# Attention sums stored unturned and normalised later; part of the row maxima copied out of PSUM by ScalarE

## The reference

```python
def _L0_attn_ref(x, Wq, Wk, Wv, bv, Wo, bo):
    ...
    q = _rope(q)
    k = _rope(k)
    scores = jnp.einsum('bhsd,bhtd->bhst', q, k) * scale
    causal = jnp.triu(jnp.ones((S, S), dtype=bool), k=1)
    scores = jnp.where(causal, -jnp.inf, scores)
    probs = jax.nn.softmax(scores, axis=-1)
    out = jnp.einsum('bhst,bhtd->bhsd', probs, v)
    out = out.transpose(0, 2, 1, 3).reshape(B, S, HID)
    return jnp.einsum('bsh,eh->bse', out, Wo) + bo

def _L0_ffn_ref(x, W_fc, W_proj):
    ...
    h = jnp.square(jax.nn.relu(jnp.einsum('bsd,fd->bsf', x, W_fc)))
    y = jnp.einsum('bsf,df->bsd', h, W_proj)
    ...
    _, spks = jax.lax.scan(step, mem0, None, length=NUM_STEPS)
    return jnp.sum(spks, axis=0) / NUM_STEPS
x = L0_attn_x
x = x + 0.5 * _L0_ffn_ref(_layernorm(x, axis=-1), L0_ffn_W_fc, L0_ffn_W_proj)
x = x + _L0_attn_ref(_layernorm(x, axis=-1), L0_attn_Wq, L0_attn_Wk, L0_attn_Wv, L0_attn_bv, L0_attn_Wo, L0_attn_bo)
x = x + 0.5 * _L0_ffn_ref(_layernorm(x, axis=-1), L0_ffn_W_fc, L0_ffn_W_proj)
```

## Time and profile before

| | |
|---|---|
| time, median of 3 runs | 1481.79 us (1480.66 to 1482.88) |
| the profiled execution | 1480.84 us, span 1479.1 us |
| PE, DVE, ACT busy | 1345.1, 1134.0, 861.4 us |
| attention's exponentials | from 405 to 1250 us; a group from 1 to 6 takes 106.0 us |

### The profile page before, as it was taken

How to read it: one execution, slowest core, us unless ns; L and a number is a source line. 1 busy time by engine, 2 the same in 40 slices (tenths; PEclk the granted TensorE clock), 3 DMA queues, 4 the chain that set the end, 5 groups by cost and what they waited for, 6 DMA issues and landing times.

```text
span 1479.1 us, 22638 instructions
## 1 busy us (share of the span) xinstructions
PE 1345.1 (91%) x8416; PEld 809.8 (55%) x8416; DVE 1134.0 (77%) x2686; ACT 861.4 (58%) x1157; POOL 223.7 (15%) x205
## 2 busy tenths in 40 slices
PE   4988888967799999999999999999999998999996
PEld 3877777854444343444444444443443433999996
DVE  6566776796788888898898898888888851576675
ACT  4654455511166666676666666666666668665664
POOL 4002222241210110110110110110210110101100
PEclk9999999976699999999999999999999999999998
DMA  3123443772272160250340420610701011232312
GB/s 110 48 81 119 136 135 122 149 209 93 72 109 29 27 92 6 39 75 6 56 59 6 75 40 5 91 24 5 106 9 44 9 33 47 76 100 87 99 44 72
DMA packets 98598, 101.41 MB, mean 69 GB/s; under 512 B 39260, under 2 KB 78940, under 8 KB 96860
## 3 DMA queue, kind: packets, MB, share of 16 engines
q1 hardware_dynamic: 98488, 99.97, 29.7%
HBM read 60.16 MB, written 37.75 MB: 66 GB/s over the span
## 4 chain that ended last, share of the span: by engine, by line
PE 74%; DVE 19%; ACT 4%; issue 3%; DMA 0%; POOL 0%; SPq 0%; DVEq 0%; ACTq 0%
PE m_ps L1049 20%; PE o_ps L1094 18%; DVE maxes L971 9%; PE yps_c L563 6%; PE ups_c L545 6%; PE s_ps L1078 5%; PE ups_a L545 5%; PE yps_a L563 4%; PE gps_a L594 3%; DVE masked L974 3%; PE gps_a L579 2%; DVE turned_a L403 2%; PE gps_c L579 2%; ACT probs L950 1%; PE tps_a L572 1%
## 5 line engine op out<-in xcount | busy, mean ns | idle before, releaser
L950 ACT ACTIVATE probs<-s_ps 128x1024 f32<-128x1024 f32 (+3 forms) x640 | 542.0, 896 | 282.6 <-PE s_ps L1078 281.2
L971 DVE TENSOR_REDUCE maxes<-m_ps 128x1 f32<-128x512 f32 x768 | 490.2, 684 | 72.6 <-PE m_ps L1049 70.7
L1049 PE MATMUL m_ps<-kT,qT 64*128 64x512 f32 (+3 forms) x1280 | 455.6, 459 | 56.4 <-DVE maxes L971 37.9
L1049 PEld LDWEIGHTS m_ps<-kT,qT 64*128 64x128 f32 x1280 | 204.2, 192 | 412.1 <-DVE maxes L971 277.6
L1078 PE MATMUL s_ps<-qT,kT 64*128 64x512 f32 (+3 forms) x1280 | 317.0, 404 | 6.8 <-ACT probs L950 6.6
L1094 PE MATMUL o_ps<-probs,v_w 128*32 128x512 f32 (+3 forms) x2560 | 311.1, 559 | 0.1
L974 DVE CUSTOM_DVE_ANT_0 masked<-m_ps,mask 128x384 f32<-128x384 f32 (+3 forms) x512 | 233.6, 485 | 52.7 <-PE m_ps L1049 50.8
L919 POOL TENSOR_SCALAR_AFFINE_SELECT probs<-probs 128x512 f32<-128x512 f32 x128 | 81.3, 635 | 742.0 <-ACT probs L950 742.0
L1078 PEld LDWEIGHTS s_ps<-qT,kT 64*128 64x128 f32 x1280 | 170.0, 192 | 34.0 <-ACT probs L950 28.7
L452 DVE TENSOR_TENSOR h_lo_c<-hsq_c,h_hi_c 128x512 fp32r<-128x512 f32 x64 | 45.0, 703 | 71.1 <-ACT hsq_c L301 35.6
L294 ACT ACTIVATE relu_a<-ups_a 128x512 f32<-128x512 f32 x64 | 38.2, 596 | 99.5 <-PE ups_a L545 98.9
(11 more groups left out here) (128 smaller groups left out, 1923.3 us busy)
## 6 DMA issues: line engine op xcount, KB each, us to landing
qT<-qkT_parts SPq DMA_DIRECT2D x96, 128.0 KB
kT<-qkT_parts SPq DMA_DIRECT2D x48, 256.0 KB
qkT_parts<-qk_hi_a SPq DMA_DIRECT2D x32, 256.0 KB, 4.9
qkT_parts<-qk_lo_a SPq DMA_DIRECT2D x32, 256.0 KB, 4.6
table_a<-in_rot SPq DMA_DIRECT2D x8, 768.0 KB, 7.4
xin_a<-in_x SPq DMA_DIRECT2D x8, 512.0 KB, 3.9
xres_a<-in_x SPq DMA_DIRECT2D x8, 512.0 KB, 4.8
x<-xsum_a SPq DMA_DIRECT2D x8, 512.0 KB, 3.2
```

The lines of the kernel that those rows point to most:

```text
L950: act.activation(probs[:, b % PBUF, 2 * hp:2 * hp + 2, off:CH], s_ps[hp][:, :, off:CH], ACT.Exp, scale=D ** -0.5).then_inc(exp_done, 1)
L971: dve.tensor_reduce(out, m_ps[:, i % MB, 0:width], AX.X, ALU.max).then_inc(max_read, 1)
L1049: pe.matmul(m_ps[:, i % MB, 0:width], qT[n % 2][r0:r0 + HR, j, hp, t * P:(t + 1) * P], kT[n % 2][r0:r0 + HR, hp, k * CH:k * CH + width], s ...
```

## The change

**The sums are no longer turned.** ACT copies `o_ps` to one of two halves of `osum`, and three slots after a step's end SP stores them as they are, head by head with queries along the row, to `sumsT`. The 32 ring items of sums go, on PE and on DVE. In the second feed-forward SP loads the denominators of a chunk as 128 x 64 numbers, DVE takes their reciprocals in one instruction (`attn_recip`), SP stores them to `recipT` and loads them back, each row repeated over its head's 16 rows (`denom`), beside the sums (`sums`); DVE multiplies the two (`attn_norm`, 128 x 1024), ACT takes the high part and DVE the low part, now from SBUF. `attn_turn` goes.

**ACT copies half of step 3's plain units.** In groups 1 to 7 the units of step 3 with k = 0 and k = 1 are copied by ACT to `copies` (`copy`, 32 a group, 224 in all); DVE reads both copies of a tile in one instruction over 1024 columns (`copied_pair`), at least two of DVE's own units after the second copy. A bank with such a unit is free once it is copied.

```diff
+COPY = [e for _, e in ORDER if e[0] == "unit" and e[1] > 0 and UNITS[e[2]][0] == NJ - 1 and UNITS[e[2]][4] <= 1]
...
+CBUF = 4
+PAIR_LAG = 2
...
+        def copy(e):
+            i, pair = ITEM[e], PAIR_NO[(e[1],) + UNITS[e[2]][:4]]
...
+            act.wait_ge(max_done, i + 1)
+            if pair >= CBUF:
+                act.wait_ge(max_read, PAIR_READ[PAIRS[pair - CBUF]])
+            act.activation(copies[:, pair % CBUF, UNITS[e[2]][4], :], m_ps[:, i % MB, :], ACT.Copy).then_inc(copied, 1)
...
+            units = [e for e in ITEMS.get(g, []) if e in COPIES]
             for hp in range(2):
+                for e in units[2 * hp:2 if hp == 0 else None]:
+                    copy(e)
                 act.wait_ge(s_done, 2 * g + hp + 1)
...
+        def copied_pair(p):
...
+            both = copies[:, pair % CBUF, :, :].rearrange("p k c -> p (k c)")
+            dve.tensor_scalar(both, both, 0.0, NEG, ALU.add, ALU.max, accum_out=maxes[:, j % 2, par, hp, t, 1:2])\
+               .then_inc(max_read, 1)
...
         def free_bank(e):
-            wait(pe, max_read, ITEM[e] if e in LATE else ITEM[e] - MB + 1)
+            if ITEM[e] >= MB:
+                last = ORDER[ITEM[e] - MB][1]
+                if last in COPIES:
+                    pe.wait_ge(copied, COPIES[last] + 1)
+                else:
+                    pe.wait_ge(max_read, READ[last])
...
-        def turn_sums(e):
...
-        def normalise(e):
...
-        def attn_turn(c):
...
+        def attn_recip(c):
+
+            wait(dve, f"denom_in{c % 2}", 16 * (c // 2 + 1))
+            dve.reciprocal(recip[:, c % 2, :], recip[:, c % 2, :]).then_inc(s["a_recip"], 1)
+
+        def attn_norm(c):
+
+            wait(dve, "a_in", 16 * 2 * EC * (c + 1))
+            dve.tensor_tensor(sums[:, :, :], sums[:, :, :], denom[:, :, :], ALU.mult).then_inc(s["a_norm"], 1)
```

More of the change, by code:

```diff
@@ L101, in feed_forward @@
     else:
-        ain, xb, x2, bias = (own[n] for n in ("ain", "xb", "x2", "bias"))
+        sums, recip, denom, xb, x2, bias = (own[n] for n in ("sums", "recip", "denom", "xb", "x2", "bias"))
         split = [("o", own["stage_o"][:, :], proj_hi, proj_lo)]
@@ L222, in body @@
                     store_x2(it + 1)
+                if has(it, -3):
+                    load_denom(it + 3)
+            elif f == FC - 1 and has(it, -3):
+                store_recip(it + 3)
         def end():
@@ L245, in high, with attn_high @@
                 wait(act, "proj_done", 3 * c)
-            if which == "a":
-                wait(act, "o_done", c)
             act.activation(hi[:, :, :], bank[:, :, :], ACT.Copy).then_inc(s[which + "_hi"], 1)
+        def attn_high(c):
+            wait(act, "a_norm", c + 1)
+            wait(act, "o_done", c)
+            act.activation(mT_hi[:, :, :], sums[:, :, :], ACT.Copy).then_inc(s["a_hi"], 1)
         def v_evac(c):
@@ L663, in body @@
                 up(it, 0)
-            if not first and f == 5 and has(it, -2):
-                attn_turn(it + 2)
         return lead, body
@@ L740 @@
 LAST_UNIT = {(e[1], UNITS[e[2]][0]): e for _, e in ORDER if e[0] == "unit"}
-LATE = [("sums", GROUPS - 1, j) for j in (NJ - 2, NJ - 1)]
-assert [e for _, e in ORDER[-2:]] == LATE
+COPY = [e for _, e in ORDER if e[0] == "unit" and e[1] > 0 and UNITS[e[2]][0] == NJ - 1 and UNITS[e[2]][4] <= 1]
+COPIES = {e: i for i, e in enumerate(COPY)}
+PAIRS = sorted({(e[1],) + UNITS[e[2]][:4] for e in COPY},
+               key=lambda p: max(COPIES[e] for e in COPY if (e[1],) + UNITS[e[2]][:4] == p))
+PAIR_NO = {p: i for i, p in enumerate(PAIRS)}
+CBUF = 4
+PAIR_LAG = 2
+PAIR_AT = {}
+for p in PAIRS:
+    second = max(ITEM[e] for e in COPY if (e[1],) + UNITS[e[2]][:4] == p)
+    at = second + 1
+    lag = 0
+    while lag < PAIR_LAG:
+        lag += ORDER[at][1][0] == "unit" and ORDER[at][1] not in COPIES
+        at += 1
+    PAIR_AT.setdefault(ORDER[at - 1][1], []).append(p)
+READ, PAIR_READ, items_read = {}, {}, 0
+for _, e in ORDER:
+    items_read += e not in COPIES
+    READ[e] = items_read
+    for p in PAIR_AT.get(e, []):
+        items_read += 1
+        PAIR_READ[p] = items_read
 TERMS = [(m, x, par) for m in range(NT) for x in range(2) for par in range(2)]
 LOADS, SHIFTS = 16 * NT * (2 + G) + 32, 16 * 4
-def bank_of(e):
-    return MB - 1 if e in LATE else ITEM[e] % MB
 def place(n):
@@ L822, in moves @@
                     shift(n, j)
-                elif what == "sums":
+            for n, j in steps():
+                if g == min(block_no(n, j, T * j + T) + STORE, LAST):
                     store(n, j)
@@ L1126, in end @@
                 products(*SLOTS[g])
-        def last_sums():
-            ring(ITEMS[LAST])
-        return slot, end, last_sums
+        return slot, end
     return sync, scalar, vector, gpsimd, tensor
```

213 lines of the change are left out of this document (113 added, 100 removed).

## The result

The changed kernel took 1633.0 us (median of 4 runs, 1631.2 to 1633.8), the kernel before 1481.3 in the same comparison: a ratio of 1.102, 95% interval 1.100 to 1.104. The direction is as predicted; 1523 us and its range of 1485 to 1550 are not. The profiled execution took 1632.59 us, span 1630.9.

What follows compares the result with a forecast made beforehand. DVE and PE, handing banks back and forth, bound slots 4 to 19; PE alone bounds the second feed-forward. 1480.8 - 21 (sums, second feed-forward) + 63 (copies) = 1523 us, range 1485 to 1550.

Steps and rivals of the forecast that it cites:

- The pair: Slots 4 to 19: DVE's read of two copies, 1024 columns, costs 1.14 us, saving 0.06 us against two plain maxima.
- Rival A: Slots 4 to 19: pair read at two columns a cycle, copies cost 39 us, kernel 1499 us; chance 0.2.
- ACT's work: Slots 4 to 19: 32 copies add 15.4 us, making 43.3 us against 41.79; 10 us over seven groups.
- ACT over 90% busy: Sign to look for in slots 4 to 19 of groups 1 to 7, with these slots 50 to 52 us long.
- The fours of slots 14 to 19: Slots 14, 16 and 18, all four units copied: four copies cost 1.4 us by the longer loop.
- The longer loop: Chain over pairs through PE and DVE, slots 16 to 18: 6.7 us for two slots against 5.33 before.
- the shorter loop: Chain over ACT, PE and DVE from slot 16's second exponential to slot 18's copy: 6.1 us for two slots.
- The step that failed: Slots 9 and 10 have room for four copies, mixed slots 4 to 8 alternate less; all copies 9 us a group.
- Rival D: Attention: PE gets one more half-speed stretch in each group, 24 us on top, 1547 us; chance 0.08.
- The sums: Attention: 32 ring items go from PE and DVE, 12 us off.
- The second feed-forward: Without attn_turn 7.2 us off, 2 more at group 7's end; DVE's added 1.5 us a chunk covered, otherwise 9 us back.
- Rival B: Slots 4 to 19: copies absorbed in ACT's idle time, only 10 us of throughput added, kernel 1470 us; chance 0.12.

Runs made afterwards that it cites:

- e13: Changed kernel with each copy in ACT's queue where its unit stands in PE's order, and full pair reads two uncopied units later in DVE's queue; 1553.1 us.
- e8: Changed kernel with copies only in slots 12 to 19, 16 a group, part of the units missing from the maxima; 1548.0 us.
- e6: Changed kernel with each copy put into ACT's queue where its unit stands in PE's order; 1605.8 us.
- e14: Changed kernel with only the full pair reads moved two uncopied units later in DVE's queue; 1619.4 us.
- e4: Changed kernel with ACT copying 64 of a unit's 512 columns and DVE reading 128 of a pair's 1024; 1546.9 us.
- e1: Changed kernel without any copies, keeping the unturned sums; 1475.6 us.
- e7: Changed kernel with every unit of scores of groups 1 to 7 computed twice into the same bank; 1672.9 us.
- e5: Changed kernel without copies and with the next tile's norm one step earlier in the second feed-forward; 1462.1 us.
- e12: Changed kernel with only the norm of the tile after next one step earlier in the second feed-forward; 1619.7 us.
- e3: Changed kernel with the read of a pair taking in only 256 columns of each copy; 1626.2 us.

## Why the prediction was right in direction and wrong in size

- **The pair.** Right. The read took 1211 ns and 82 for its accumulator; neighbours start 1.14 us apart (648.93 and 650.07), the price taken. Rival A falls. The rule that the Trainium skill gives in "VectorE: DVE Perf Modes", Mode 2x_2P, does not hold for this form, and the exclusion that the Trainium skill states in "SBUF — State Buffer", "Who interferes with whom", agrees with the measured 1211 ns. `attn_norm` took 1.22 us as priced, the reciprocals 0.55 us where 0.25 was taken.
- **ACT's work.** Right in its sum. The sum of 43.3 us for slots 4 to 19 compares with 26.86 + 16.83 = 43.7 busy in e13. What the prediction wanted to see in the changed kernel, ACT over 90% busy, was not there: 65% in slots 4 to 13. By its own test the step failed there, and e13 shows the state that it had assumed (95%).
- **The fours of slots 14 to 19.** Right in their sum, partly by luck. The longer loop was 6.7 us for two slots; slots 16 and 17 took 6.75 in groups 1 to 7, and 6.21 with half pairs (the shorter loop: 6.1). But in groups 1 to 6 slots 14 and 15 took 7.8 and slots 18 and 19 6.5, and the 5.33 us of before, from which the cost was counted, were the mean of 5.0 and 5.66. Three fours were priced at 3 x 1.4 = 4.2 us, measured 1.9 + 1.7 + 0.9 = 4.5, and e8 shows the same slots up to 2 us longer.
- **The step that failed.** "One of them lies in slots 9 and 10, where the exponentials are narrow and ACT has room ... the mixed slots 4 to 8 alternate less than the others." Slots 4 to 13 were thus priced at about 5 us. They cost 17.8, that is 13 us a group or some 90 of the 110 us missed. Slots 8 to 11, with the four copies of slots 9 and 10 that were to be free, doubled from 7.7 to 15.7 us. Slot 4, counted with the mixed ones, has four copies itself. A mixed slot alternates more, not less: ACT's queue has copies ahead of exponentials whose units come behind the products, and DVE's queue has two reads of pairs ahead of masked maxima that PE needs. I had traced only two loops, in the slots where all four units are alike. e6 and e14 show each of the two orders as a loss in these slots, and e13, with both mended, took 28.3 us in them where the changed kernel took 43.0 and before 25.2. Its sixteen slots, 46.2 to 47.6 us, lie below the 50.8 forecast; what it loses besides lies in slots 20 to 23, for which the prediction had no term.
- **The clock.** Rival D was the right kind: more time at half speed. In slots 4 to 19 the changed kernel had 2 x (0.28 x 42.98 + 0.07 x 21.10) = 27 us at half speed a group, where D had one stretch of 6.7 more. What one costs can be read where one kernel's equal groups differ, from the windows of e4, slots 4 to 19 of groups 2 and 3:

```profile
634.14:688.03 53.89, 47.29 (x256) 18.15 (x255) 21.63 (x85) 33.36 (x65) 4.90 (x5) 0.81 0.42 63
750.27:800.75 50.48, 43.55 (x256) 16.68 (x255) 21.62 (x85) 33.37 (x65) 4.89 (x5) 0.90 0.45 68
```

  20.5 us at half speed against 10.1, and 3.4 us longer: 0.33 us each. By that, as an estimate, 27 us cost 9 of the 22.3 us that a group lost, some 60 in seven groups, against the 24 of D. Other equal groups give 0.1 us each (e13, groups 2 and 3) to 0.4 (e14, groups 1 and 2; e1, slots 20 to 23), so the 9 may be 3 or 11. e7 shows that the clock isn't lifted by giving PE more to do. In e13, with most waits gone, 27 us at half speed became 0 to 10. So the clock enlarges the loss, and by these prices it is not the larger part of it.
- **The sums.** Group 0, which has no copies, got 2.7 us shorter (forecast: some 2), 1.5 of it in slots 24 to 27, where the clock was 0.87 for 0.77. The 12 us for all of attention are neither confirmed nor refuted: from the first exponential to the last, attention is 14.4 us shorter in e1's profile and 27.9 in e5's, whose attention is the same code; in e1 slots 20 to 23 of four groups took 12.4 us at a clock of 0.72, in e5 9.7 at 1.00. The price of the items is thus mixed with the clock, and which part is which stays open.
- **The second feed-forward.** Wrong. "Some 1.5 us in 27, beside PE" took for granted that what DVE gains in work costs nothing. The cover held on DVE and failed on ACT, which waits for the norm. Forecast were 9 us off behind attention; it became 10 us longer, and e12 takes off 12.7, which leaves 2.7 of the 9. From 9 off to 10 on is 19 us, nearly all that the slots 4 to 13 leave of the 110 missed. The prediction had named the price of a lost cover, 9 us; measured, 13.3.
- **Chances.** Rival B, absorbed copies, had 0.12, and no kernel with full copies came near it: ACT fills the sixteen slots, 43.7 of 46.2 us, even in the best order. "The rest of a group shrinks by more than 3 us" did not occur (2.0).

Left open: why slots 14 to 19 of e6 took 24.1 us against 21.1 in the changed kernel, where the other 6 of the 9 us behind attention went, and what sets a half-speed stretch off.

## What to carry to other kernels

When work moves to an engine with idle time, price its place in that engine's queue before its duration: for each instruction added, ask which one stands behind it and whether what it waits for comes later than what that one waits for. Trace one such path for every kind of slot, the mixed ones first, not for the regular ones alone. Where three engines wait for one another and none of them is full, look for order. Narrowing one suspect at a time can clear them all (7 us and 5 us here), where both together, or a new order, show the loss (86 and 80 us). And read such trials by the slots that they touch, not by the kernel's time alone: e14's 14 us hid a gain of 9 us a group in one place behind a loss of 7 in the next.

## What the hardware showed that I had not expected

- One program's equal groups did not run alike: e4's groups 1 to 6 took 50.5, 51.7 or 53.9 us in slots 4 to 19, with 10, 14 or 20 us of them at half speed. e1's ten runs spread over 1464 to 1481 us, before's thirteen beside them over 1480 to 1487.
- Halving the reads of pairs (e3) raised PE's time at half speed: the clock over slots 4 to 13 of group 2 was 0.65, against 0.72 in the changed kernel. Less work for DVE went with more of PE's time at half speed, though PE was busier by its records (84% of these slots for 76%). Nothing here says why.
- Reads of a pair, `tensor_scalar` with an accumulator, are recorded as TENSOR_SCALAR_CACHE_REDUCE, with an accumulator read of 82 ns that the next instruction overlaps.
